# A gated layer's last product in two-part float16: three of four layers, order string otherwise kept

## The reference

```
x = x + 0.5 * int8_linear(norm(x))       # layer 0
x = x + attention0(norm(x))              # layer 1: 16 heads of width 8, causal
x = x + 0.5 * int8_linear(norm(x))       # layer 2
x = x + 0.5 * gated(norm(x))             # layer 3
x = x + attention1(norm(x))              # layer 4: 16 heads of width 64, causal
x = x + 0.5 * gated(norm(x))             # layer 5

def gated(x):                            # whole-number weights, each times 1/127
    h = silu(x @ wg.T) * (x @ wu.T)      # 128 -> 384
    return h @ wd.T                      # 384 -> 128
```

## Time and profile before

| | |
|---|---|
| three runs | 791.9, 794.64, 794.64 us; median 794.64 |
| the profiled execution | 794.18 us, of which 792.4 us from the first to the last instruction |
| mean granted TensorE clock | 0.961 of full speed |
| busy: PE, PEld | 724.7 us (91%), 431.6 us (54%) |
| busy: DVE, ACT, POOL | 534.4 us (67%), 454.5 us (57%), 466.6 us (59%) |
| chain that ended last | PE 74%, DVE 12%, ACT 9% |

### The profile page before, as it was taken

The page is one execution under the profiler, slowest core; times in us unless marked ns, Lnnn a source line. Parts: engine busy times, 40 slices in busy tenths (PEclk is TensorE's granted clock), DMA queues, the critical chain, the costliest instruction groups (busy, mean ns, idle before and its releaser), DMA issues.

```text
span 792.4 us, 21544 instructions
## 1 busy us (share of the span) xinstructions
PE 724.7 (91%) x9387; PEld 431.6 (54%) x9387; DVE 534.4 (67%) x739; ACT 454.5 (57%) x534; POOL 466.6 (59%) x367
## 2 busy tenths in 40 slices
PE   2767888888888899999999999999999999999997
PEld 1633445444444554566556566555666555656774
DVE  7598888889998685668775675655655565453337
ACT  2325667889775779555646545555534656646202
POOL 6726446125542300489979849885861898877530
PEclk9756899999999999999999999999999999999999
DMA  8000000000000000001101101100110110111100
GB/s 272 2 1 2 3 2 3 2 4 2 2 3 2 2 2 3 2 3 29 28 3 29 29 2 31 27 10 24 29 29 2 29 29 2 29 29 30 29 27 27
DMA packets 13226, 16.20 MB, mean 20 GB/s; under 512 B 3053, under 2 KB 10573, under 8 KB 13133
## 3 DMA queue, kind: packets, MB, share of 16 engines
q1 hardware_dynamic: 12556, 14.50, 6.5%
q10 hardware_dynamic: 576, 0.33, 0.1%
HBM read 13.26 MB, written 1.17 MB: 18 GB/s over the span
## 4 chain that ended last, share of the span: by engine, by line
PE 74%; DVE 12%; ACT 9%; issue 3%; POOL 1%; DMA 1%; ACTq 0%; DVEq 0%; POOLq 0%
PE ps L1261 19%; PE ps L1210 17%; DVE big L1074 7%; ACT Pr L697 7%; PE ps L1181 6%; PE ps L1425 5%; PE ps L1240 5%; PE ps L1464 3%; PE ps L1432 3%; PE ps L1382 2%; PE ps L1271 2%; PE ps L1376 1%; PE ps L1251 1%; PE ps L1231 1%; PE ps L1221 1%
## 5 line engine op out<-in xcount | busy, mean ns | idle before, releaser
L697 ACT ACTIVATE Pr<-ps,exp_scale 128x1024 f32<-128x1024 f32 (+1 forms) x285 | 277.4, 1029 | 132.4 <-PE ps L1261 68.9
L679 POOL TENSOR_TENSOR V0s<-V0s,Pr 128x1024 f32<-128x1024 f32 x77 | 181.3, 2354 | 92.6 <-PE ps L1210 65.1
L1105 DVE TENSOR_REDUCE mxb<-ps 128x8 f32<-128x1024 f32 (+1 forms) x154 | 173.7, 1151 | 85.0 <-PE ps L1261 55.4
L1074 DVE TENSOR_REDUCE big<-ps 128x8 f32<-128x1024 f32 (+1 forms) x164 | 171.3, 1089 | 27.7 <-PE ps L1240 20.1
L1261 PE MATMUL ps<-big 64*128 64x128 f16 (+2 forms) x2560 | 171.0, 260 | 0.2 <-ACT Pr L697 0.2
L1240 PE MATMUL ps<-big 32*128 32x128 f16 (+2 forms) x1280 | 103.7, 279 | 34.8 <-DVE big L1074 16.1
L1261 PEld LDWEIGHTS ps<-big 64*128 64x128 f16 x2560 | 92.6, 94 | 76.9 <-issue 28.8
L1210 PE MATMUL ps<-Pr,V1s 128*64 128x128 f32 (+2 forms) x960 | 112.8, 372 | 0.1
L1240 PEld LDWEIGHTS ps<-big 32*128 32x128 f16 x1280 | 43.5, 96 | 108.5 <-ACT Pr L697 40.3
L679 POOL TENSOR_TENSOR acts<-acts,Pr 128x1024 f32<-128x1024 f32 x35 | 83.2, 2378 | 22.2 <-PE ps L1210 10.8
L1181 PE MATMUL ps<-Pr,V0s 128*18 128x128 f32 (+2 forms) x1280 | 80.8, 380 | 0.0
(11 more groups left out here) (242 smaller groups left out, 920.5 us busy)
## 6 DMA issues: line engine op xcount, KB each, us to landing
rec_b<-scratch_dram SPq DMA_DIRECT2D x30, 256.0 KB, 3.9
X<-in_x_dram SPq DMA_DIRECT2D x2, 256.0 KB, 3.5
big<-in_pick_rows_dram SPq DMA_DIRECT2D x2, 256.0 KB, 3.5
X<-in_x_dram SPq DMA_DIRECT2D x1, 512.0 KB, 5.9
rec_b<-in_w_q_dram SPq DMA_DIRECT2D x1, 512.0 KB, 6.1
XT<-in_w_k_dram SPq DMA_DIRECT2D x1, 512.0 KB, 6.8
XT<-in_w_v_dram SPq DMA_DIRECT2D x1, 512.0 KB, 7.9
wo_s<-in_w_o_dram SPq DMA_DIRECT2D x1, 512.0 KB, 8.5
```

The source lines that it names most:

```text
L679: g.tensor_tensor(dst, dst, src, ALU.add).then_inc(summed, 1)
L697: ins = a.activation(dst[:, part], src, func, scale=scale)
L1074: ins = v.tensor_reduce(maxima_of(mall[:, r, 2 * u:2 * u + 2][:, part], i), block_view(src, i), AX.X, ALU.max, negate=True)
L1105: ins = v.tensor_reduce(maxima_of(mxb[:, r][:, part], arg), block_view(src, arg), AX.X, ALU.max, negate=True)
```

## The change

- Steps: each of the layers (3,0), (3,1), (5,0) gets six "split" steps. Split k stands behind up k+1 (the last two behind up 5), so the letter `h` appears 18 times more in `ORDER`; without the split steps the list is the old one, step for step, with the same banks.
- DVE writes up k's result into a ring `ffn_t` of three float32 buffers, and from k = 3 waits for the low part of k-3.
- ACT copies it to float16 (the high part). Then the difference, float32 minus high part, is written as float16 (the low part): by POOL in layer (3,0), by DVE in layers (3,1) and (5,0) (`LOW_ON_V`).
- `down` waits for the last low part and issues 48 float16 matmuls, two for each of before's 24.
- In the prelude POOL converts the gate and up weights in two operations instead of one, the up weights with a factor of 2**-14, and makes a float16 copy `wd_16` of the whole-number down weights last.
- The final factors follow, and `dynamic_dma_scratch_size=1024` is passed when the program is made; the program's transfers are all issued by SP and ACT.

```diff
+TERMS = 3
+H_SCALE = 2.0**-14
+LOW_ON_V = ((3, 1), (5, 0))
...
 def gated_steps(s, b):
-    return (turned_norm_steps(s, b) + [("up", (s, b), (c, half), "AV") for c in range(HC) for half in range(2)]
-            + [("down", (s, b), None, "V")])
+    ups = [[("up", (s, b), (c, half), "AV"), ("split", (s, b), 2 * c + half, "")] for c in range(HC) for half in range(2)]
+    woven = ups[0][:1] + [step for k in range(1, len(ups)) for step in (ups[k][0], ups[k - 1][1])] + ups[-1][1:]
+    return turned_norm_steps(s, b) + woven + [("down", (s, b), None, "V")]
...
-            g.tensor_copy(wg_s[:], raw_gu)
+            g.tensor_copy(wg_s[:, 0], raw_gu[:, 0])
+            g.tensor_scalar(wg_s[:, 1], raw_gu[:, 1], H_SCALE, None, ALU.mult)
             g.tensor_scalar(wd_s[:], raw_d, W_SCALE, None, ALU.mult).then_inc(converted, 1)
...
             g.memset(tops(1), SHIFT_TOP).then_inc(slots_set, 1)
+            g.tensor_copy(wd_16[:], raw_d).then_inc(converted, 1)
...
+                if kind == "split" and key not in LOW_ON_V:
+                    c, half = divmod(arg, 2)
+                    pool.wait_ge(h_high, SPLIT_NO[key, arg] + 1)
+                    g.tensor_tensor(ffn_16[:, 1, c, half_of(half)], ffn_t[:, arg % TERMS], ffn_16[:, 0, c, half_of(half)],
+                                    ALU.subtract).then_inc(h_low, 1)
...
+                if kind == "split":
+                    c, half = divmod(arg, 2)
+                    act.wait_ge(slot_dve, read("V", "up", key, (c, half)))
+                    a.activation(ffn_16[:, 0, c, half_of(half)], ffn_t[:, arg % TERMS], ACT.Copy).then_inc(h_high, 1)
...
-                    v.tensor_tensor(ffn_h[:, c, 512 * half:512 * half + 512], gate, slot[1],
-                                    ALU.mult).then_inc(slot_dve, 1)
+                    if 2 * c + half >= TERMS:
+                        dve.wait_ge(h_low, SPLIT_NO[key, 2 * c + half - TERMS] + 1)
+                    v.tensor_tensor(ffn_t[:, (2 * c + half) % TERMS], gate, slot[1], ALU.mult).then_inc(slot_dve, 1)
+                if kind == "split" and key in LOW_ON_V:
+                    c, half = divmod(arg, 2)
+                    dve.wait_ge(h_high, SPLIT_NO[key, arg] + 1)
+                    v.tensor_tensor(ffn_16[:, 1, c, half_of(half)], ffn_t[:, arg % TERMS], ffn_16[:, 0, c, half_of(half)],
+                                    ALU.subtract).then_inc(h_low, 1)
...
                 if kind == "down":
-                    pe.wait_ge(slot_dve, read("V", "up", key, (HC - 1, 1)))
+                    pe.wait_ge(h_low, SPLIT_NO[key, GATED - 1] + 1)
+                    pe.wait_ge(converted, 2)
                     for t in range(T):
                         for h in range(HC):
-                            ins = te.matmul(tile_of(slot, t), ffn_h[:, h, tile(t)], wd_s[:, h], start=h == 0,
-                                            stop=h == HC - 1)
+                            for w in range(2):
+                                ins = te.matmul(tile_of(slot, t), ffn_16[:, w, h, tile(t)], wd_16[:, h],
+                                                start=(h, w) == (0, 0), stop=(h, w) == (HC - 1, 1))
```

More of the change, by code:

```diff
@@ L120, in summed_columns @@
     return view[:, :, :, a % every:a % every + z - a]
+GATED = 2 * HC
+TERMS = 3
+H_SCALE = 2.0**-14
+LOW_ON_V = ((3, 1), (5, 0))
 GROUP_BUFS = 6
@@ L188 @@
     "emwemewemegmewewemmhwemeemtemewemewmemwhmemwemmemwemgeemwhmmmhheewehmhewmamewemhewemewemetmhemwmemwm"
[L189 to L195, removed]
+    "ememwmeewmhemheawmehmeehwewmememewmhemwemgeewmmhetwmmhhhhhhhhhhhheewemheewehwmeewmeemewmegeemwemhewm"
+    "mhwemmKKQtQVweMeeMwMeewMegeweMeweMeweMeweMeweMeweeTQKwwMMgEEEMWMEMWWMMWEEEEMWWhWMEMhTVhMQKWhhEMWMEEE"
+    "SWWMEEMWMMWWMEEMWTWMhEQKVEWhMWMEMWMEEEMWMEMSMEMWMhTEhEVQVhKhWEWWWMMMWWEEEWMMhWWMEMWMEMWMSTEMWMEEWMMK"
+    "EWWEMVhWWEEhQTWShhhhWEEMMWWMEEEhhhhhhhWWQKhMEWMEMWEMMWhEEhMWEMEWMMVTSEMMWWEMMWWEVhWEEEMWWWMEESTEEQKW"
+    "WMMMWWWEEMWMEMWMEEEEMWSEMQVKTWWWMWEEEMWMMWWMEEMWQKVSWWMEEVMMWWEEMTWMEEMWWMEMWMMEWMWSEEKOQEEWEMEMEMWM"
+    "WVMTOWWMMOQMOSEMKWWEEMEhWWMEMWWETWMEEMWMWMEMWEMWMEEEhEWWKVQTSEWWEMWMEEMWMMMWWMEWMEEEKVQVWEMMWWMEEEMW"
+    "WTMMSWWWEMQKEWEMMWEMMWEEEEEhVWSTWWWWMEEMWMWEMMWWMEEEMWSEEEEMWWWWThhhhhWWEEEEWEEEOhhOEWWWWSEOhhhhhOhW"
+    "WWW"
 )
@@ L201 @@
 READS = {e: list(accumulate(int(e in step[3]) for step in PLAN)) for e in "AV"}
+SPLIT_NO = {step[1:3]: n for n, step in enumerate([step for step in PLAN if step[0] == "split"])}
 NORM_NO = {step[1]: n for n, step in enumerate([step for step in PLAN if step[0] == "ln" and step[2] == 0])}
@@ L265, in macaron_block_kernel @@
         ffn_g = sb("ffn_g", [P, 2, 512])
+        ffn_t = sb("ffn_t", [P, TERMS, 512])
+        ffn_16 = ffn_h[:, :, :].rearrange("p c s -> p (c s)").bitcast(F16).rearrange("p (w c s) -> p w c s", w=2, c=HC)
         W = ffn_h[:, HC - 1].rearrange("p (t c) -> p t c", t=T)
@@ L291, in macaron_block_kernel @@
         wd_s = sb("wd_s", [P, HC, P])
+        wd_16 = sb("wd_16", [P, HC, P], F16)
         id_s = sb("id_s", [P, P])
@@ L389, in macaron_block_kernel @@
                                                             sem("ln_peak"), sem("ln_out"))
+        h_high, h_low = sem("h_high"), sem("h_low")
         bias_added, int_added = sem("bias_added"), sem("int_added")
@@ L1041, in _ @@
                         at = in_banks(X[:, b].rearrange("p t c -> p (t c)"))[:, part]
-                        ins = v.scalar_tensor_tensor(at, src, 1.0 if kind == "wo0" else 0.25 * W_SCALE**2, at, ALU.mult, ALU.add)
+                        ins = v.scalar_tensor_tensor(at, src, 1.0 if kind == "wo0" else 0.25 * W_SCALE**3 / H_SCALE, at,
+                                                     ALU.mult, ALU.add)
                     ins.then_inc(slot_dve, 1)
@@ L1163, in _ @@
                 dve.wait_ge(last_down, half + 1)
-                v.scalar_tensor_tensor(at, bank(1 + half).rearrange("p (t c) -> p t c", t=4), 0.25 * W_SCALE**2, at,
+                v.scalar_tensor_tensor(at, bank(1 + half).rearrange("p (t c) -> p t c", t=4), 0.25 * W_SCALE**2 / H_SCALE, at,
                                        ALU.mult, ALU.add).then_inc(last_x, 1)
@@ L1595 @@
     arrays.update(_constants())
-    nc = bacc.Bacc("TRN2", target_bir_lowering=False, num_devices=1)
+    nc = bacc.Bacc("TRN2", target_bir_lowering=False, num_devices=1, dynamic_dma_scratch_size=1024)
     args = [nc.dram_tensor(f"in_{n}_dram", a.shape, mybir.dt.from_np(a.dtype), kind="ExternalInput").ap()
```

## The result

The changed kernel takes 801.42 us, the median of 4 runs (800.82 to 804.78), beside 793.27 for the kernel before on the same chip: a ratio of 1.0122, with an interval of 1.0089 to 1.0155. In a second comparison it was 804.20 beside 792.72: 1.0151 [1.0103, 1.0199]. So it is slower by some 10 to 12 us.

A forecast was written before the change was run, and what follows sets the result against it. PE was taken as the bound from about 300 to 762 us. Terms -0.15 + 3.1 + 0.45 + 3.3 + 0 gave +6.7 us: 794.18 became 800.9, and 0.46 more for the median gave 801.3; range 795 to 806.

The forecast's parts named there:

- What `down` saves: In each layer's `down`, 48 float16 matmuls take 2.7 us instead of 5.36: some 2.7 us saved, 8.1 in all.
- Layer (3,0): Low parts on POOL, no lock; `down` starts 2.55 us later through ACT's queue, less 2.7 saved: -0.15 us.
- the loss of 0.3 us in the ups: In (3,0), ACT's copy and tanh make the last four ups come some 0.3 us late in all.
- The idle 2.5 us: Sign in (3,0): PE idle some 2.5 us ahead of `down`, released by ACT.
- Layer (3,1): Low parts on DVE wait for POOL's adds; `down` starts 5.8 us later, less 2.7 saved: +3.1 us.
- the list: In (3,1), the predicted times of low parts, maxima, exps and ups, ending with `down` at 460.45 instead of 454.66.
- Layer (5,0): Ups 0 to 2 cost +0.45 us; `down` starts 4.9 to 7.1 us later, less 2.7 saved, taken as +3.3.
- the middle between low 5 at once and low 5 behind the waiting add: In (5,0), low 5 done at 756.6 or 758.9; net +2.2 to +4.4 us, taken as +3.3.
- The lock itself: A DVE low part with two SBUF inputs meeting POOL's running add waits for its end, done 0.55 us later.
- the 2.9 that I named as a sign: Sign in (3,1) and (5,0): POOL adds recorded for 2.9 us beside DVE's low parts.
- The prelude and `wd_16`: POOL's scaled conversion gains 0.4 or loses 0.65 us, taken as 0; `wd_16` falls in 19.7 us of POOL idleness.

The follow-up runs named there:

- e5: The kernel before with float16 `down` alone: DVE writes float16 at once, no copies or low parts, high part read twice; 786.37 us, ratio 0.9921.
- e3: The changed kernel with 15 and 32 filler matmuls on PE ahead of `down` in (3,1) and (5,0); 801.86 us, ratio 1.0111.
- e3b: The changed kernel with 8 and 32 filler matmuls on PE ahead of `down` in (3,1) and (5,0); 798.25 us in one run.
- e6: The changed kernel's full computation with the order of ups and split steps rearranged in all three layers; 797.70 us, ratio 1.0076.
- e7: As e6, but layer (3,1) left in float32 with its places of before; 793.59 us, ratio 1.0002.
- e8: The changed kernel, but layer (3,1) left in float32 with its places of before; 799.52 us, ratio 1.0097.
- e1: The changed kernel with DVE's subtraction in (3,1) and (5,0) replaced by a reduction with one SBUF input, no low part there; 793.14 us, ratio 0.9999.

## Why the prediction came out as it did

The sign, the mechanism of the lateness and nearly each start were right; the sum was 5.4 us short of the stages' 12.1, and the early clock of the profiled pair hid 4.6 of that. Of the 5.4 some 4.6 are PE's clock in the three `down` steps, which no term held; the rest is starts.

- **What `down` saves** (48 x 0.056 = 2.7 us each): right at full clock, 2.84 us beside 5.5, shown by e5. In the changed kernel it failed: all three took 4.3 to 4.4 us in the first profile, and 2.85, 4.47 and 4.82 in the second. This is the term that was mis-sized. I priced a wait of PE as its length, and left out what the clock takes afterwards: behind 3.50 and 7.04 us of waiting it stood at 0.62, and 1.6 us of the 2.7 were gone. e3 shows it by filling the wait with matmuls.
- **Layer (3,0)**, forecast -0.15, measured +0.7 in one profile and -0.7 in the other. `down` came 2.0 us later, not 2.55: the loss of 0.3 us in the ups did not occur, since they kept their pace of 1.32 us with ACT's copy and tanh overlapping by 0.1, and exps 6/0 took a little less. The rest, 1.4 us, is the clock: 0.50 in 256 to 262 of the first profile, 1.00 in the same work of the second. Its wait there is short (0.55 us), and I have no cause for it; all other profiles with these places had the full clock. The idle 2.5 us that I forecast ahead of `down` was 0.96 and 0.77 in the second profile.
- **Layer (3,1)**, forecast +3.1, measured +4.8. `down` starts 32.5 us behind `xt` instead of 26.6: +5.9, forecast +5.8. Low 0, low 1, the three maxima, up 3 and lows 2 to 5 came within 0.3 us of the list, once it is shifted by the earlier start. Of the 1.7 that is missing 1.6 is the clock.
- **Layer (5,0)**, forecast +0.45 and +3.3, measured +6.6. `down` starts 7.8 us later in its stage, forecast 6.45. Ups 0 to 2 cost 0.7 instead of 0.45 (up 4 starts 57.6 us behind `xt`, before 56.9). I had taken the middle between low 5 at once and low 5 behind the waiting add; it was the add, 1.1 us more, in every profile that has two low parts in sequence beside waiting adds (the change twice, e3, e3b, e6, e7, e8). The clock is 1.6 more. The Trainium skill ("SBUF — State Buffer", "Who interferes with whom") has the order of issue decide who gets the shared read interface; the rows at 757.06 and 739.31 agree, and with it the term would have been +4.4. The middle between two ends was the wrong choice where a rule named one.
- **The lock itself**: right, and by its own number, 0.55. The adds that had to let a low part through were recorded for 2.6 us, not for the 2.9 that I named as a sign. The rule of the same section of the Trainium skill, that a DVE instruction with one SBUF input is not held up, was not in the prediction's sum; e1's 0.68 beside the same adds agrees.
- **The prelude and `wd_16`**: taken at nothing. A begins at 247.0 in the kernel before and at 242.0 to 248.2 in the changed ones, so an effect of less than that spread would not be seen.
- **What I would have needed for +12**: PE's clock behind each wait, and order of issue. Both were bounds that I could have set: the profile before had no late `down`, but it had windows at half clock.

The timed ratio of the first comparison, +9.7 us, is 3 above my sum, with an interval from +7.1 to +12.3 that leaves the sum out; the second is +12.0. That 801.3 stands so near the median of 801.42 is partly chance: it was built on 794.64 us for the kernel before, which took 793.27 in the comparison, with 4 runs of either kernel and a coin worth some 5 us in each. The forecast of the time was met with the help of luck; the sum behind it was too low.

## What to carry to other kernels

Before an operation with two SBUF inputs goes onto DVE, look at what POOL does in that place: beside this kernel's stream of adds it cost what was left of the running add and 0.55 us, and the second of two in a row waited for a whole further add; with one input from SBUF it cost its own 0.7 us. Where an in-order engine is the bound, a longer chain ahead of one of its steps wants other work of that engine in between, and PE's wait is to be priced with the slower stretch behind it. Rearranging is not free either: the steps put in between must not be the late engine's own.

## What the runs showed of the hardware that was not expected

- Behind waits of 3.1 to 10.2 us PE ran 48 float16 matmuls in 4.4 to 5.3 us instead of 2.84. In e8 the same wait of 7.05 us as in the change was followed by 5.3 us where the change had 4.42 (first profile, 7.04) and 4.82 (second, 7.05):

```profile
754.80:760.10 5.30, 5.30 (x50) 5.10 (x52) 0.08 (x1) 0.00 (x0) 1.95 (x1) 0.50 0.00 0
```

  The clock is at its lower level, 1.2 GHz, throughout this one, and for part of the others. The Trainium skill ("TensorE: Matmul & The Clock Gate", "HAM oscillation — how this bites in real kernels") tells of a matmul kernel whose PE falls back to the lower clock in each wait for data; here that agrees for all eight `down` steps behind waits of 3.1 to 10.2 us, while e1's waits of 1.57 and 2.09 us left the clock at 1.00. The slow `down` of (3,0), behind a wait of 0.55 us, is explained by neither.
- The clock between 90 and 100 us is 0.6, 0.8 or 1.0 from one profile to the next; where it is 0.58 to 0.66 stage A begins at 246.3 to 248.2, where it is 0.83 or 1.00 at 242.0 to 243.2. A difference between two single profiles has to be read stage by stage.
- A POOL add that waited for DVE is recorded longer by some 0.2 us (2.58 to 2.60 beside 2.36), and in all profiles every low part on DVE that waited for POOL ends 0.54 to 0.56 us behind it.
